# Attention in a decoder layer: fewer small VectorE operations, and another order of the steps on VectorE and GpSimd

## The reference, cut to what matters

```python
q = rmsnorm(rope(h @ w_qc @ w_qup)) * g_qnorm      # 8 heads of 64, rope on the first 32
k = rmsnorm(rope(h @ w_k)) * g_knorm               # one head for all
v = h @ w_v
comp = softmax([scores on 2 block means of k, sink])   # then @ block means of v
sel  = softmax(causal scores) @ v                      # no sink
sw   = softmax([causal scores, sink]) @ v              # the same scores, with the sink
g = sigmoid(q @ w_gate + b_gate); g = g / max(sum(g), 1e-6)
mixed = g[0] * comp + g[1] * sel + g[2] * sw
y = per-group product of mixed, then @ w_out
x1 = (x + y - mean) / sqrt(var + 1e-5)
```

## Time and profile before

| | before |
|---|---|
| median of 3 runs | 769.38 us |
| the profiled execution's own time | 767.93 us |
| its span | 766.1 us |
| VectorE busy in the span | 554.0 us (72%) |
| TensorE, ScalarE, GpSimd busy | 566.3, 444.2, 460.7 us |
| the attention stage | up to about 300 us of the span |

### The profile page before, as it was taken

One profiled execution on the slowest core, in us unless ns is written; L12 is line 12 of the kernel. 1 busy time (PEld: TensorE's weight loads), 2 busy tenths in 40 slices (PEclk: granted clock), 3 DMA queues, 4 the chain that ended last, 5 costly groups with the idle time before them and its releaser, 6 DMA issues.

```text
span 766.1 us, 17009 instructions
## 1 busy us (share of the span) xinstructions
PE 566.3 (74%) x4773; PEld 430.0 (56%) x4773; DVE 554.0 (72%) x1891; ACT 444.2 (58%) x1363; POOL 460.7 (60%) x553
## 2 busy tenths in 40 slices
PE   4766777777777775797998897873109898989864
PEld 2444555555555554465676665552008888888831
DVE  2589999999999985368688988963406666666514
ACT  2588777878787772496687565430005555555515
POOL 4568777777777753555556487778741444445533
PEclk9999889999998897598999999885559999999998
DMA  6144444531111111200111111011111222122164
GB/s 233 55 161 174 172 149 145 179 122 34 34 44 33 37 31 31 73 26 22 36 40 40 36 54 33 29 50 46 53 45 50 66 58 71 53 70 61 37 204 130
DMA packets 69468, 57.78 MB, mean 75 GB/s; under 512 B 22133, under 2 KB 64250, under 8 KB 67074
## 3 DMA queue, kind: packets, MB, share of 16 engines
q1 hardware_dynamic: 64450, 46.14, 19.5%
q0 software_dynamic: 4352, 8.47, 3.3%
q10 hardware_dynamic: 576, 2.10, 0.7%
HBM read 25.86 MB, written 31.33 MB: 75 GB/s over the span
## 4 chain that ended last, share of the span: by engine, by line
PE 19%; issue 17%; POOL 15%; DMA 3%; DVE 3%; ACT 2%; SPq 1%; POOLq 0%; ACTq 0%; DVEq 0%
PE ps L1300 8%; POOL l_keys L957 6%; POOL disp_dram L982 5%; PE ps L1325 4%; PE ps L1306 2%; PE ps L1336 2%; POOL l_rs L964 2%; POOL x_xr L969 2%; DMA l_R<-y_dram 1%; PE ps L1280 1%; DMA out_x<-l_keys 1%; ACT l_keys L1398 1%; POOL y_dram L1409 1%; POOL l_W1l L973 1%; PE ps L827 1%
## 5 line engine op out<-in xcount | busy, mean ns | idle before, releaser
L1409 POOL DMA_INDIRECT y_dram<-l_keys,m_blk x72 | 70.5, 979 | 97.2 <-ACT l_keys L1376 83.2
L350 ACT ACTIVATE a_E<-a_ps,a_nb,a_sc 128x64 f32<-128x64 f32 x256 | 99.6, 408 | 10.6 <-DVE a_nb L473 9.6
L431 POOL TENSOR_TENSOR a_rinv<-a_ms,a_halfneg 128x9 f32<-128x9 f32 x32 | 57.7, 1803 | 33.4 <-DVE a_ms L546 33.4
L309 PE MATMUL a_ps<-a_tab,a_xTt 128*128 128x512 f32 x64 | 38.9, 692 | 46.9 <-DVE a_r L488 41.5
L982 POOL DMA_INDIRECT disp_dram<-l_R,x_pos x64 | 62.9, 983 | 17.5 <-issue 17.3
L957 POOL TENSOR_TENSOR l_keys<-x_kT,l_table 128x1024 f32<-128x1024 f32 x32 | 62.0, 1937 | 6.7 <-ACT x_kT L906 6.4
L1441 DVE TENSOR_SCALAR m_lin<-ps 128x512 f32<-128x512 f32 x36 | 24.9, 691 | 49.5 <-PE ps L1306 48.4
L964 POOL TENSOR_TENSOR l_rs<-x_ve,l_halfneg 128x2 f32<-128x2 f32 x32 | 23.9, 748 | 57.2 <-DVE x_ve L1113 56.9
L350 ACT ACTIVATION_READ_ACCUMULATOR a_E<-a_ps,a_nb,a_sc 128x1 f32 x256 | 53.3, 208 | 0.0
L1376 ACT ACTIVATE l_keys<-ps,m_blk 128x128 f32<-128x128 f32 x72 | 22.6, 364 | 44.1 <-PE ps L1325 43.5
L1022 DVE TENSOR_SCALAR l_R<-x_r,x_mv,l_rs 128x256 f32<-128x256 f32 x32 | 20.3, 635 | 35.1 <-POOL l_rs L964 27.7
(11 more groups left out here) (234 smaller groups left out, 1943.8 us busy)
## 6 DMA issues: line engine op xcount, KB each, us to landing
disp_dram<-l_R SPq DMA_DIRECT2D x16, 1040.0 KB, 4.2
m_blk<-disp_dram SPq DMA_DIRECT2D x72, 65.0 KB
a_xTt<-in_xT SPq DMA_DIRECT2D x32, 64.0 KB, 3.8
l_W1l<-in_w SPq DMA_DIRECT2D x1, 2048.0 KB
a_VB<-v_dram SPq DMA_DIRECT2D x128, 16.0 KB, 2.0
a_xt<-in_x SPq DMA_DIRECT2D x32, 64.0 KB, 2.0
x_dram<-a_xo SPq DMA_DIRECT2D x32, 64.0 KB, 1.7
x_xa<-x_dram SPq DMA_DIRECT2D x32, 64.0 KB, 1.9
```

The costliest lines, as they stand in the source:

```text
L309: nc.tensor.matmul(flat[:, 0:512], xTt[:, a.u2, :], wqkv[:, 0:512], start=True, stop=True)
L350: last = nc.scalar.activation(E[:, e.u4, g, :], ps_Sh[:, g // 4, g % 4, 0:D], ACT.Exp, bias=nb[:, e.u2, g:g + 1], scale=sc8[:, e.u4, g:g + 1],
L431: G.tensor_tensor(rinv[:, b.u4, :], ms[:, b.u2, :], halfneg[:, 0:9], ALU.pow).then_inc(inv_rms, 1)
L1409: G_.indirect_dma_start(out=Y[:, :], out_offset=bass.IndirectOffsetOnAxis(ap=blk[:, (2 * q + j) % NB, P:P + 1].bitcast(I32), axis=0), in_= ...
```

## The change

On VectorE some operations become one: the sink's logit is kept as the third column of `u3`, so that one reduction gives the maximum `mc` and one subtraction gives three arguments; the sum of the exponentials is written by ScalarE straight into `den`; and the weights come from products of denominators, with one reciprocal, instead of products of reciprocals. The factor 1/8 is folded into `gg` and (as the same scale of k) out of the score's scale, so that `sc8`, `root` and `scales` go. The two sine products on GpSimd become one with a reversed view. The norm's variance plus epsilon is written as a tenth column behind the nine mean squares, and one power of ten columns gives both; where there is no tile s-1 any more, the norm has a power of its own. VectorE's step has another order: scores, residual sum, sum of squares, statistics, block means, variance; then `xo`, block scores, ropes, arguments, normed k; the weights last. GpSimd's step does the power before the mixing products.

```diff
@@ scalar
                     e.free(act, mixed, 4)
+                    e.free(act, mixing, 2)
...
-                                                    bias=nb[:, e.u2, g:g + 1], scale=sc8[:, e.u4, g:g + 1],
-                                                    accum_out=Z[:, e.u2, g:g + 1])
+                                                    bias=nb[:, e.u2, g:g + 1], scale=rinv[:, e.u4, g:g + 1],
+                                                    accum_out=den[:, e.u2, g, 1:2])
@@ gpsimd
-                    G.tensor_tensor(tb[:, :, 0:16], q[:, :, 16:32],
-                                    sin[:, 0:16].unsqueeze(1).to_broadcast([P, 9, 16]), ALU.mult)
-                    G.tensor_tensor(tb[:, :, 16:32], q[:, :, 0:16],
-                                    sin[:, 16:32].unsqueeze(1).to_broadcast([P, 9, 16]),
+                    G.tensor_tensor(tb[:, :, :].rearrange("p h (w k) -> p h w k", w=2),
+                                    q[:, :, 0:32].rearrange("p h (w k) -> p h w k", w=2)[:, :, ::-1, :],
+                                    sin[:, :].rearrange("p (w k) -> p w k", w=2).unsqueeze(1).to_broadcast([P, 9, 2, 16]),
                                     ALU.mult).then_inc(sined, 1)
...
+                if k.live:
+                    k.wait(pool, ln_var)
+                if k.live and not b.live:
+                    G.tensor_tensor(rs[:, k.u2:k.u2 + 1], ve[:, :], halfneg[:, 0:1], ALU.pow).then_inc(ln_rstd, 1)
+                if b.live:
+                    b.wait(pool, mean_sq)
+                    b.free(pool, exped, 4)
+                    b.free(pool, x1_done, 11)
+                    w = 10 if k.live else 9
+                    G.tensor_tensor(rinv[:, b.u4, 0:w], ms[:, b.u2, 0:w], halfneg[:, 0:w],
+                                    ALU.pow).then_inc(inv_rms, 1)
                 if f.live:
                     f.wait(pool, mixing)
...
-                if k.live:
-                    k.wait(pool, ln_var)
-                    G.tensor_tensor(rs[:, k.u2, :], ve[:, k.u2, :], halfneg[:, 0:1], ALU.pow).then_inc(ln_rstd, 1)
-                if b.live:
-                    b.wait(pool, mean_sq)
-                    b.free(pool, exped, 4)
-                    G.tensor_tensor(rinv[:, b.u4, :], ms[:, b.u2, :], halfneg[:, 0:9], ALU.pow).then_inc(inv_rms, 1)
-                    b.wait(pool, inv_rms)
-                    G.tensor_tensor(sc8[:, b.u4, :], rinv[:, b.u4, 0:H], root[:, :], ALU.mult).then_inc(scales, 1)
@@ vector (the new order, after nb; the same operations left out of their old places)
+                if k.live:
+                    k.wait(dve, y_done)
+                    k.wait_ring(dve, x_in, 16)
+                    k.free(dve, x1_done, 2)
+                    V.tensor_tensor(r[:, k.u2, :], ps_y, xt[:, k.u2, :], ALU.add).then_inc(y_added, 1)
+                if b.live:
+                    b.wait(dve, squared)
+                    n_ss = n.add(V.tensor_reduce(ss[:, :], sq[:, b.u2, :, :], AX.X, ALU.add))
+                if k.live:
+                    k.wait(dve, y_added)
+                    n_bn = n.add(V.bn_stats(st[:, :], r[:, k.u2, :]))
+                if b.live:
+                    n.upto(n_ss)
+                    b.free(dve, inv_rms, 2)
+                    V.tensor_scalar(ms[:, b.u2, 0:9], ss[:, :], 1.0 / D, 1e-6, ALU.mult, ALU.add).then_inc(mean_sq, 1)
+                if k.live:
+                    n.upto(n_bn)
+                    n_mv = n.add(V.bn_aggr(mv[:, k.u2, :], st[:, :]))
+                if d.live:
+                    d.wait(dve, kT_copied)
+                    V.tensor_reduce(KB[:, d.u2, :, :, 64:66], ...
+                if k.live:
+                    n.upto(n_mv)
...
+                    V.tensor_scalar(ms[:, b.u2, 9:10] if b.live else ve[:, :], mv[:, k.u2, 1:2], 1e-5, None,
+                                    ALU.add).then_inc(ln_var, 1)
+                if l.live:
+                    inv_std, done, count = rstd(l.t)
+                    dve.wait_ge(done, count)
...
@@ vector (arguments)
-                    n_mc = n.add(V.tensor_tensor(mc[:, :], un[:, :, 0], un[:, :, 1], ALU.max))
+                    n_mc = n.add(V.tensor_reduce(mc[:, :], u3[:, :, :], AX.X, ALU.max))
...
-                    n_mc = n.add(V.tensor_tensor(mc[:, :], mc[:, :], snk[:, :], ALU.max))
...
-                    n.add(V.tensor_tensor(arg[:, e.u2, :, 0:2], un[:, :, :],
-                                          mc[:, :].unsqueeze(2).to_broadcast([P, H, 2]), ALU.subtract))
-                    n_arg = n.add(V.tensor_tensor(arg[:, e.u2, :, 2], snk[:, :], mc[:, :], ALU.subtract))
...
+                    n_arg = n.add(V.tensor_tensor(arg[:, e.u2, :, 0:3], u3[:, :, :],
+                                                  mc[:, :].unsqueeze(2).to_broadcast([P, H, 3]), ALU.subtract))
@@ vector (weights, new)
+                    n_dg = n.add(V.tensor_scalar(dg[:, :, :], ex[:, f.u2, :, 4:7], 1.0, None, ALU.add))
+                    n.add(V.tensor_reduce(den[:, f.u2, :, 0], ex[:, f.u2, :, 0:3], AX.X, ALU.add))
+                    n_den = n.add(V.tensor_tensor(den[:, f.u2, :, 2], den[:, f.u2, :, 1], ex[:, f.u2, :, 3], ALU.add))
+                    n.upto(n_dg)
+                    n_rdg = n.add(V.reciprocal(rdg[:, :, :], dg[:, :, :]))
                     n.upto(n_den)
+                    n.add(V.tensor_tensor(dd[:, :, :], den[:, f.u2, :, :], dg[:, :, :], ALU.mult))
+                    n.upto(n_rdg)
+                    n.add(V.tensor_reduce(gs[:, :], rdg[:, :, :], AX.X, ALU.add))
+                    n.settle()
+                    n.add(V.scalar_tensor_tensor(dd[:, :, :], gs[:, :].unsqueeze(2).to_broadcast([P, H, 3]), 1e-6,
+                                                 dd[:, :, :], ALU.max, ALU.mult))
+                    n.settle()
+                    n.add(V.reciprocal(wt[:, :, :], dd[:, :, :]))
+                    n.settle()
                     f.free(dve, mixed, 2)
+                    n.add(V.tensor_tensor(pa[:, f.u2, :], wt[:, :, 1], wt[:, :, 2], ALU.add))
```

## The result

The changed kernel takes 869.54 us (median of 4 runs) against 769.63 for the kernel before on the same chip: a ratio of 1.1295, interval 1.1268 to 1.1321. It is slower, as forecast, but by 100 us and not by 52: outside the range of 804 to 846. The profiled execution has a span of 868.9 us.

The account below looks back on a forecast made before the run. VectorE bounds the kernel before; afterwards a loop through GpSimd's moved power does. Its 10.11 us plus 0.2 for clock give 10.3 a step, +46.4 us over 25 steps; with head and tail +51.9, so 821 us, range 804 to 846.

Parts of the forecast that it names:

- The bound before and the loop: VectorE sets the old 8.45 us step; the moved power closes a loop through TensorE, VectorE and GpSimd.
- The loop at full clock: TensorE 3.81, VectorE 1.86, power 1.95, products 2.25 and releases 0.24 us: a step of 10.11 us.
- part 4: TensorE's clock: idle of about 3.6 us a step can but need not lower it; 0.2 us a step added.
- both rows: Earlier trace: transposes at 1.2 GHz after 3.81 us idle; mask products at 2.4 GHz after 3.37 us idle.
- The second row: Earlier trace at 40.38: two mask products take 0.39 us, the 2.4 GHz duration, after 3.37 us of idle.
- the clock falls in most steps: Rival on TensorE's clock: 845 us if half the steps are hit fully, 874 us if all; chance 0.16.
- The power: GpSimd's power of ten elements takes 1.95 us, within bounds of 1.80 and 2.41.
- part 3: GpSimd's power moved ahead of the mixing products closes a loop of 10.11 us, against a step of 8.45.
- The sum: 25 full attention steps at 10.3 us give 257.5 against 211.1 us; with head and tail, +51.9 us.
- The last steps: The five shorter attention steps after the full ones, 30.12 us before, grow by 4 us.
- VectorE's reorder hidden: The rest of VectorE's new order ends near 11 us, before the next scores at 12.5: hidden by 1.5 us.
- part 1: VectorE's fewer instructions and two held operations gone or moved: its step falls from 8.45 to about 5.9 us.

Follow-up runs that it names:

- run 1: The changed kernel with GpSimd's power and its two waits put back behind the two mixing products; 716.74 us, ratio 0.9476 to the kernel before.
- run 2: The kernel before with only GpSimd's powers and scaling moved ahead of its two mixing products; 911.59 us, ratio 1.2008.
- run 3: The changed kernel with twenty unread mask products added at the end of TensorE's step; 798.93 us, ratio 1.0525 to the kernel before.
- run 7: The changed kernel with only the mean squares' power ahead of the products, the variance's behind, and VectorE's sum of squares before the residual sum; 751.22 us, ratio 0.9908.
- run 5: The changed kernel again, unmodified, in a later series; 859.27 us, ratio 1.1207 to the kernel before.
- run 6: The changed kernel with two powers, the mean squares' ahead of the mixing products and the variance's behind them; 817.19 us, ratio 1.0772 to the kernel before.
- run 10: The changed kernel with the power behind the mixing products and the normalized rows `xo` first on VectorE; 714.05 us, ratio 0.9425 to the kernel before.

## Why the prediction was wrong, point by point

1. The bound before and the loop: right. In the changed kernel the transposes wait for GpSimd, VectorE waits ahead of the maximum (105.3/25, 4.2 us a step), the power starts at the variance and the products behind it. Run 1 and run 2 show that the place of the power alone turns a gain into the loss.
2. The loop at full clock: forecast 10.11 us, measured 9.60 (run 3). TensorE's part was taken with a gap behind the transposes that belonged to the old step (3.81 for 3.58), the products with half a hold (2.25 for 2.16), and the way from y to the power as 2.02 us with two releases (1.84).
3. The step that failed is part 4, the clock: "I add 0.2 per step". It measured 2.04. I had both rows, one in which the products behind idle time ran at 1.2 GHz and one in which they didn't, and priced the risk of a fall as one in twelve. With 3.3 to 3.9 us idle in EVERY step it came in every step: of the 25, not one had its TensorE part at 3.8 us. And I had overlooked how often it came in the kernel before. The second row itself is at 1.2 GHz, 1.11 us for the transposes behind only 2.24 us of idle time, and in the full steps, whose granted clock of 0.91 stands in the earlier trace rows, the product with v is slow in every second step, behind 2.2 us of idle time two lines above it:

```profile
177.98 1.18 PE L309 MATMUL a_ps<-a_tab,a_xTt 128*128 128x512 f32 x2 [2.24 <-DVE a_r L488]
178.95 0.64 PE L310 MATMUL a_ps<-a_tab,a_xTt 128*128 128x128 f32 x2
179.38 1.91 PE L317 MATMUL a_ps<-a_PT,a_VB 128*128 128x256 f32 x4
...
187.69 1.03 PE L317 MATMUL a_ps<-a_PT,a_VB 128*128 128x256 f32 x4
```

   The rival "the clock falls in most steps" had given 874 us for the fall in all steps and a chance of 0.16; that is the case that came, less its full price (5.62 on the mean for 6.11), since the steps got back to 2.4 GHz before y or within it. The Trainium skill's rule ("TensorE: Matmul & The Clock Gate", HAM oscillation: a recurring wait makes each group of matmuls start throttled) stood in the prediction and was right for this wait; the trace agrees, with transposes of 1.06 to 1.12 us in 22 of the 25 steps where 0.66 is their length at 2.4 GHz. The prediction put it without the length of the wait: 1.56 us in every step of run 7 and 1.02 in run 3 left the clock at 2.4 GHz.
4. The power: forecast 1.95, measured 2.00 or, in 16 of the 25 steps, 2.45. That is 0.3 us a step over 2.00, and in part 3's sum the one term that was too low. That the products might hold VectorE was seen; that something might lengthen the power wasn't. What does is argued with run 5.
5. The sum: 25 x (9.60 + 2.04 + 0.3) = 298.5 us, against 298.91 measured. The forecast had 257.5; the 41 missing are 46 of clock (25 x 1.84, since 0.2 was in it) and 7.5 of hold, less 12.8 for the loop taken too long: that the loop came out too long hid part of the miss by luck. The last steps gave 10 instead of 4 us; their clock is 0.75 against 0.85 before, but no run separates its share.
6. VectorE's reorder hidden: right, no step waits for it. The gain that part 1 put at 2.5 us of a step isn't reached when nothing hides it: 8.45 to 6.96 in run 1. Part 1's 5.9 us for VectorE's step was too low: its busy time is 6.4 us a step in the changed kernel and 6.8 in run 1, where it hardly ever waits and other operations are held in place of the old ones (`xo` 0.81 us for 0.34).

## What to carry to other kernels

In a pipeline of in-order engines, before moving a wait ahead of an operation, follow who uses that operation's result one step later, and back round to the wait: if the path closes within one step, the step can't be shorter than it. A loop that leaves TensorE idle in every step is to be priced from rows with a like idle time in every step. Here 2.8 us (run 6), 3.3 to 3.9 (the changed kernel) and 5.2 us (run 2) went with a TensorE part of about 5.0 us or more in at least 24 of 25 steps, and 1.0 and 1.6 us (runs 3 and 7) with 3.58. And an input merged into a shared operation comes only when the last of the merged ones does.

## What the runs showed that I had not expected

- Idle filled with products that nobody reads (20 of them, 2.5 us a step) took 6 to 7% off the kernel's time (ratio 1.0525 against 1.1295 and 1.1207), since the clock stayed at 2.4 GHz and the powers at 2.00 us.
- A 10-column power on GpSimd takes 1.96 to 2.09 us in most runs, but 2.26 or 2.27 in all full steps but the first of run 10 and 2.45 in 16 of 25 steps of the changed kernel, in 2 of 25 when it ran again. The lengths go with the start of a 0.45 us two-input product of VectorE beside it; that this is the cause is argued.
- An operation of one tensor input on VectorE is held too: `xo` takes 0.33 us by itself, and 0.81 in the runs where it starts while GpSimd multiplies.
